# A decoder block in fp32 on one core: products weighed together per step, and an opening group in two halves of 256 tokens

## What is computed

```python
qkv = x @ w_atten.T                      # x: (4, 512, 512), normalised over its features
q, k = apply_rope(q, rope), apply_rope(k, rope)
att = jnp.einsum('bhqd,bhkd->bhqk', q, k) * (1.0 / jnp.sqrt(jnp.float32(D)))
att = jax.nn.softmax(jnp.where(causal, att, -inf), axis=-1)
y = jnp.einsum('bhqk,bhkd->bhqd', att, v)
return y @ w_proj.T
...
x = x + _L0_attn_ref(_layernorm(x), ...)
x = x + _L0_xattn_ref(_layernorm(x), ctx_1024, ...)
x = x + _L0_ffn_ref(_layernorm(x), ...)
```

## Time and profile before

| what | us |
|---|---|
| median of 3 runs | 1121.15 (1120.68 to 1123.51) |
| the profiled execution | 1121.97 |
| its span, first to last instruction | 1120.2 |
| TensorE busy | 1032.6 (92%) |
| VectorE busy | 600.2 (54%) |
| ScalarE busy | 482.6 (43%) |
| POOL busy | 180.6 (16%) |

### The profile page before, as it was taken

One profiled execution on the slowest core, in us unless ns is written; L12 is line 12 of the kernel. 1 busy time (PEld: TensorE's weight loads), 2 busy tenths in 40 slices (PEclk: granted clock), 3 DMA queues, 4 the chain that ended last, 5 costly groups with the idle time before them and its releaser, 6 DMA issues.

```text
span 1120.2 us, 17685 instructions
## 1 busy us (share of the span) xinstructions
PE 1032.6 (92%) x6000; PEld 735.6 (66%) x6000; DVE 600.2 (54%) x1592; ACT 482.6 (43%) x1265; POOL 180.6 (16%) x204
## 2 busy tenths in 40 slices
PE   6577799999999999999889999989999999999998
PEld 3243454564545555555454778888888988889997
DVE  3345556675567765566556455824444334443665
ACT  1144565564554655545564223213344334442221
POOL 2111111122011111111100000101111111112342
PEclk9878899999999999999999999999999999999999
DMA  6664444316443355404623103164442444423554
GB/s 188 129 106 57 57 58 70 48 27 74 106 57 78 36 71 119 57 28 50 135 76 102 33 19 104 39 237 141 145 149 92 149 152 152 144 83 94 181 170 159
DMA packets 66153, 111.21 MB, mean 99 GB/s; under 512 B 5984, under 2 KB 26976, under 8 KB 66080
## 3 DMA queue, kind: packets, MB, share of 16 engines
q1 hardware_dynamic: 60480, 91.92, 35.4%
q0 software_dynamic: 5600, 18.35, 5.5%
HBM read 59.66 MB, written 25.43 MB: 76 GB/s over the span
## 4 chain that ended last, share of the span: by engine, by line
PE 68%; DVE 12%; DMA 10%; issue 5%; ACT 2%; POOL 2%; SPq 1%; DVEq 0%; ACTq 0%; POOLq 0%
PE ps L1122 20%; PE ps L1132 10%; DMA ks<-rope_b 8%; PE ps L886 8%; PE ps L928 5%; PE ps L951 3%; PE ps L968 3%; PE ps L1026 3%; PE ps L905 3%; PE ps L917 3%; DVE gu_lo L1414 2%; PE ps L1140 2%; PE ps L988 1%; DMA routed_x<-xn_d,table_cur 1%; PE ps L1110 1%
## 5 line engine op out<-in xcount | busy, mean ns | idle before, releaser
L1265 DVE CUSTOM_DVE_ANT_0 probs<-ps,mask 128x128 f32<-128x128 f32 (+3 forms) x256 | 123.8, 487 | 140.0 <-PE ps L917 126.5
L677 ACT COPY probsT<-ps 128x128 f32<-128x128 f32 (+3 forms) x256 | 108.8, 425 | 192.0 <-PE ps L928 190.0
L917 PE MATMUL ps<-ks,qs 96*128 96x256 f32 (+2 forms) x256 | 149.4, 586 | 33.9 <-DMA ks<-rope_b 23.9
L669 ACT ACTIVATE probs<-probs,nb 128x128 f32<-128x128 f32 (+3 forms) x256 | 145.7, 569 | 34.0 <-DVE nb L1270 33.1
L886 PE MATMUL ps<-xnT,wa_sb 128*128 128x512 f32 x256 | 129.3, 620 | 3.6 <-DVE rope_b L1248 3.0
L928 PE MATMUL ps<-ident,probs 128*128 128x128 f32 x640 | 120.3, 288 | 0.1
L773 ACT ACTIVATE sg<-ps 128x352 f32<-128x352 f32 x69 | 32.0, 464 | 168.4 <-PE ps L1122 167.6
L917 PEld LDWEIGHTS ps<-ks,qs 96*128 96x128 f32 x256 | 50.9, 199 | 79.2 <-issue 36.6
L1541 DVE TENSOR_TENSOR hidden<-sg,ps 128x352 f32<-128x352 f32 x69 | 35.8, 519 | 122.8 <-ACT sg L773 122.8
L928 PEld LDWEIGHTS ps<-ident,probs 128*128 128x128 f32 x640 | 77.1, 144 | 33.7 <-issue 28.7
L570 POOL TENSOR_TENSOR rope_a<-rope_a,sin_sb 128x512 f32<-128x512 f32 x32 | 40.8, 1274 | 347.3 <-DVE rope_a L1247 347.3
(11 more groups left out here) (157 smaller groups left out, 1908.6 us busy)
## 6 DMA issues: line engine op xcount, KB each, us to landing
gu_raw<-in_we SPq DMA_DIRECT2D x10, 1408.0 KB
y_d<-y_sb SPq DMA_DIRECT2D x37, 256.0 KB
qs<-rope_b SPq DMA_DIRECT2D x32, 256.0 KB, 5.1
ks<-rope_b SPq DMA_DIRECT2D x32, 256.0 KB, 7.5
shared_x<-xT_d SPq DMA_DIRECT2D x32, 256.0 KB
d_raw<-in_we SPq DMA_DIRECT2D x10, 512.0 KB
qs<-rope_a SPq DMA_DIRECT2D x16, 256.0 KB, 7.2
ks<-rope_a SPq DMA_DIRECT2D x16, 256.0 KB, 8.4
```

The lines of the kernel that those rows point to most:

```text
L669: nc.scalar.activation(pr, pr, ACT.Exp, bias=nb[:, n % 2, h:h + 1], scale=SCALE, accum_out=sums[:, n % 2, h:h + 1]).then_inc(exp_done, 1)
L677: nc.scalar.copy(probsT[n % 2][:, h, 0:w], ps[:, T_BANK + h % 2, 0:w]).then_inc(pT_done, 1)
L917: nc.tensor.matmul(ps[:, S_BANK + h % 2, 0:w], qs[:, G % 2, h, i * P:(i + 1) * P], ks[:, G % 2, h, 0:w], start=True, stop=True).then_inc(s ...
L1265: nc.vector.tensor_tensor_reduce(probs[n % TT][:, h, 0:w], ps[:, S_BANK + h % 2, 0:w], mask[:, TOKENS - w:], 1.0, LOWEST, ALU.add, ALU.max ...
```

## The change

Four things. **Weighing**: `weigh(n)` now does all blocks of a step at the place of head 1 (`WEIGH_HEAD`), where one block stood at each place from head 0 on. **The opening** works on tokens 0 to 255 and then 256 to 511: x tiles 0 and 1, both first weights and tables, then x tiles 2 and 3 on the queue; statistics, root, turning, projections, rope and stack in halves; value tile 0 alone ahead of the loop, tiles 1 to 3 on places 0 to 11. The stack of each half counts on a semaphore of its own; scores of step 0 wait for the first, those of step 2 for the second. **Places and banks of groups 1 to 4**: their queries and keys stand close together (`EARLY_QUERIES`, `EARLY_KEYS`), keys in a bank other than the queries'; the sums of group 1 stand on places 6 and 8, those of groups 2 and 3 on the second and fourth place of the group ahead of theirs, those of group 4 on places 49 and 51. In the later batches value tile 3 comes three places earlier. **The stack** of every group: the high parts are sent when they are cast (`rope_high`), the low part when it is there (`rope_done`). All parts of the weights stand in front of the first stack, as before; the loads that stood behind it now stand behind the stacks of groups 1 (second x), 2 (weights, biases, context) and 3 (third x).

```diff
+WEIGH_HEAD = 1
...
-VALUES = ((-5, -5, -3, -3), (8, 9, 10, 10), (11, 12, 12, 14), (27, 27, 28, 29))
-VALUE_COPIES = (-3, 10, 14, 29)
+VALUES = ((-5, -5, -3, -3), (8, 9, 10, 10), (11, 12, 12, 14), (24, 24, 25, 26))
+VALUE_COPIES = (-3, 10, 14, 26)
+
+EARLY_QUERIES = {1: (2, 2, 3, 3), 2: (-2, -2, -1, -1), 3: (-2, -2, -1, -1), 4: (45, 45, 46, 46)}
+EARLY_KEYS = {1: (4, 4, 5, 5), 2: (0, 0, 1, 1), 3: (0, 0, 1, 1), 4: (47, 47, 48, 48)}
+EARLY_RAW = {1: (4, 6), 2: (0, 2), 3: (0, 2), 4: (47, 49)}
+EARLY_SUM = {1: (6, 8), 2: (2, 4), 3: (2, 4), 4: (49, 51)}
+FIRST_VALUES = ((-1, -1, -1, -1), (0, 0, 1, 1), (7, 7, 8, 8), (10, 10, 11, 11))
+FIRST_VALUE_COPIES = (-1, 1, 9, 12)
...
-        FIRST_QK_BANKS = (QK_BANK, O_BANK)
-        FIRST_VALUE_BANKS = (T_BANK, T_BANK + 1, QK_BANK)
-        EARLY_VALUES = len(FIRST_VALUE_BANKS)
+        HALVES = (slice(0, TOKENS // 2), slice(TOKENS // 2, TOKENS))
+        FIRST_QK_BANKS = ((QK_BANK, O_BANK), (T_BANK, T_BANK + 1))
+        FIRST_VALUE_BANKS = (T_BANK, T_BANK + 1, QK_BANK, O_BANK)
+
+        def qk_bank(G, i):
+
+            if i and G <= GROUPS:
+                return O_BANK if G == 1 else X_BANK
+            return QK_BANK
+
+        def qk_places(G):
+
+            if G <= GROUPS:
+                return EARLY_QUERIES[G], EARLY_KEYS[G]
+            return (QUERIES, KEYS) if G % GROUPS else (FIRST_QUERIES, FIRST_KEYS)
+
+        def unit(G, i, half=0):
+
+            return 2 * G + i + 2 if G else 2 * half + i
+
+        def value_places(b):
+
+            return (FIRST_VALUES, FIRST_VALUE_COPIES) if b == 0 else (VALUES, VALUE_COPIES)
...
-            def stack_part(G, i):
-
-                stacks, parts = ((qs, (rope_b, rope_b, rope_a)), (ks, (rope_b, rope_a, rope_b)))[i]
-                sp.wait_ge(rope_done, 2 * G + i + 1)
-                for j, part in enumerate(parts):
-                    sp.dma_start(stacks[j * HDIM:(j + 1) * HDIM, G % 2, :, :].bitcast(F32),
-                                 part[i][:]).then_inc(stacked, 16)
+            def stack_high(G, i, half=0, cols=slice(0, TOKENS), done=stacked):
+
+                sp.wait_ge(rope_high, unit(G, i, half) + 1)
+                for j in ((0, 1), (0, 2))[i]:
+                    sp.dma_start((qs, ks)[i][j * HDIM:(j + 1) * HDIM, G % 2, :, cols].bitcast(F32),
+                                 rope_b[i][:, cols]).then_inc(done, 16)
+
+            def stack_low(G, i, half=0, cols=slice(0, TOKENS), done=stacked):
+
+                j = (2, 1)[i]
+                sp.wait_ge(rope_done, unit(G, i, half) + 1)
+                sp.dma_start((qs, ks)[i][j * HDIM:(j + 1) * HDIM, G % 2, :, cols].bitcast(F32),
+                             rope_a[i][:, cols]).then_inc(done, 16)
...
+            def load_wa(part):
+
+                first_col, past = WA_PARTS[part]
+                sp.dma_start(wa_sb[:, :, first_col:past], wa_v[:, :, first_col:past]).then_inc(wa_loaded[part], 16)
+
+            for t in range(TT // 2):
                 sp.dma_start(acc[:, t, :], x_v[0][:, t, :]).then_inc(x_loaded[t], 16)
-            wa_v = waT.rearrange("(c p) n -> p c n", p=P)
-            for part, (first_col, past) in enumerate(WA_PARTS):
-                sp.dma_start(wa_sb[:, :, first_col:past], wa_v[:, :, first_col:past]).then_inc(wa_loaded[part], 16)
-                if part == 1:
-                    sp.dma_start(cos_sb[:], cosT).then_inc(tables_loaded, 16)
-                    sp.dma_start(sin_sb[:], sinT).then_inc(tables_loaded, 16)
-            for i in range(2):
-                stack_part(0, i)
-            load_x(1)
...
+            load_wa(0)
+            load_wa(1)
+            sp.dma_start(cos_sb[:], cosT).then_inc(tables_loaded, 16)
+            sp.dma_start(sin_sb[:], sinT).then_inc(tables_loaded, 16)
+            for t in range(TT // 2, TT):
+                sp.dma_start(acc[:, t, :], x_v[0][:, t, :]).then_inc(x_loaded[t], 16)
+            for part in (2, 3, 4):
+                load_wa(part)
+            for half, done in enumerate((stacked_first, stacked)):
+                for i in range(2):
+                    stack_high(0, i, half, HALVES[half], done)
+                    stack_low(0, i, half, HALVES[half], done)
             X3_PLACE = 2 * PLACES + 18
             WEIGHTS_PLACE = group_start(ALL_GROUPS - 1) + ROPE_SUM[1]
             for place in range(DRAINED):
-                for G, i in units_at(place, FIRST_ROPE_SUM, ROPE_SUM):
-                    stack_part(G, i)
+                for G, i in units_at(place, EARLY_SUM, FIRST_ROPE_SUM, ROPE_SUM):
+                    stack_high(G, i)
+                    stack_low(G, i)
+                if place == group_start(1) + EARLY_SUM[1][1]:
+                    load_x(1)
+                if place == group_start(2) + EARLY_SUM[2][1]:
+                    for dst, src in ((wp_sb[:], wpT.rearrange("(c p) n -> p c n", p=P)),
...
+                                     (bias_sb[:, 0:1], bq), (bias_sb[:, 1:2], bk)):
+                        sp.dma_start(dst, src).then_inc(w_loaded, 16)
+                    load_context(0)
+                if place == group_start(3) + EARLY_SUM[3][1]:
+                    load_x(2)
...
+                times_sine(0, 0, half, HALVES[half])
+                times_sine(0, 1, half, HALVES[half])
+                low_of_sum(0, 0, half, HALVES[half])
+                low_of_sum(0, 1, half, HALVES[half])
...
+                        before = (G - 1, 1) if bank == X_BANK else (0, 1) if bank == O_BANK else (G, 0)
+                        pe.wait_ge(rope_raw, 2 * unit(*before) + 2)
...
+                        before = (unit(0, 0, 1), unit(0, 1, 1), unit(1, 0), unit(1, 1))[t]
+                        pe.wait_ge(rope_raw, 2 * before + 2)
...
+                if n == 0 and h == 0:
+                    pe.wait_ge(stacked_first, STACK)
+                if h == 0 and (i == 0 and G or n == 2):
...
-            def weigh(n, j):
+            def weigh(n):
 
                 G, i = divmod(n, TT)
                 b, g = divmod(G, GROUPS)
-                if j == 0:
-                    pe.wait_ge(pT_done, GH * n + GH)
-                    if i == 0 and G >= 1:
-                        pe.wait_ge(yT_done, G)
-                if g == 0 and j == i:
-                    pe.wait_ge(v_done, b * TT + j + 1)
...
-                if j == i:
-                    last.then_inc(pv_mm, 1)
+                pe.wait_ge(pT_done, GH * n + GH)
+                if i == 0 and G >= 1:
+                    pe.wait_ge(yT_done, G)
+                if g == 0:
+                    pe.wait_ge(v_done, b * TT + i + 1)
+                for j in range(i + 1):
+                    v = value_tile(b, j)
+                    for h in range(GH):
+                        last = nc.tensor.matmul(ps[h * HDIM:(h + 1) * HDIM, O_BANK, i * P:(i + 1) * P],
+                                                v[:, g, h * HDIM:(h + 1) * HDIM],
+                                                probsT[n % 2][:, h, j * P:(j + 1) * P],
+                                                start=(j == 0), stop=(j == i), skip_group_check=True)
+                last.then_inc(pv_mm, 1)
...
+            for half in range(2):
+                for t in (2 * half, 2 * half + 1):
+                    if half:
+                        pe.wait_ge(norm1.copied, t - 1)
+                    turn_tile(norm1, 0, t, X_BANK + t % 2)
+                pe.wait_ge(norm1.copied, 2 * half + 2)
+                for i in range(2):
+                    pe.wait_ge(wa_loaded[i], 16)
+                    project_qk(0, i, range(CC), FIRST_QK_BANKS[half][i], HALVES[half])
             pe.wait_ge(wa_loaded[2], 16)
-            for t, bank in enumerate(FIRST_VALUE_BANKS):
-                values(0, t, range(CC), bank)
+            values(0, 0, range(CC), FIRST_VALUE_BANKS[0])
...
-                if n is not None and h <= n % TT:
-                    weigh(n, h)
+                if n is not None and h == WEIGH_HEAD:
+                    weigh(n)
...
+                    dve.wait_ge(stacked_first, STACK)
...
+            def first_stats(half):
+
+                tiles = range(2 * half, 2 * half + 2)
+                for t in tiles:
+                    dve.wait_ge(x_loaded[t], 16)
+                    pass_wait(dve)
+                    tile_stats(norm1, 0, t)
+                dve.wait_ge(norm1.stats_made, 4 * half + 2)
                 pass_wait(dve)
-                tile_stats(norm1, 0, t)
-            variances(norm1, 0)
-            for t in range(TT):
+                for t in tiles:
+                    nc.vector.bn_aggr(norm1.mv[:, t, :], norm1.stats[:, t, :]).then_inc(norm1.stats_made, 1)
+                dve.wait_ge(norm1.stats_made, 4 * half + 4)
+                at = slice(2 * half, 2 * half + 2)
+                nc.vector.tensor_scalar(norm1.veps[:, at], norm1.mv[:, at, 1], EPS, None, ALU.add).then_inc(norm1.var_made, 1)
+
+            first_stats(0)
+            for t in range(2):
                 scale(norm1, 0, 0, t)
+            first_stats(1)
```

(12 more changed lines are left out.)

147 lines of the change are left out of this document (65 added, 82 removed).

## The result

| | before | after |
|---|---|---|
| median, us | 1120.91 (4 runs) | 1083.49 (4 runs, 1078.21 to 1085.78) |
| ratio, with its 95% interval | | 0.966 (0.9617 to 0.9703) |
| profiled execution / its span | 1121.97 / 1120.2 | 1078.21 / 1076.4 |
| TensorE busy | 1032.6 | 1010.6 |
| TensorE not busy | 87.6 | 65.8 |

The change is worth 37 us by the medians; the forecast was 1078. Half of these is time in which TensorE stood still (21.8 us), and half (22.0 us) is TensorE's own busy time. Of busy time the prediction had only some 5 us: the half clock that it took out of groups 1 to 3 (7.0 us), less 1.6 for one start.

The account below looks back on a forecast made before the run. Latency sets the time up to S4, TensorE's own work behind it. Gains of 35.9 (to S4), 7.0 (weighing) and 1.3 (last batch's stack), 44.2 from 1121.97 us, give 1078 us; range 1068 to 1090, chance 0.60.

Parts of the forecast that it names:

- S0: First scores of group 0, ending the opening: forecast at 22.9 us, 15.0 earlier than before.
- group 0: From the first scores of group 0 to those of group 1: 29.0 us, with the next stack's transfer finishing last.
- group 1: From its first scores to those of group 2: 23.5 us, two equal limits, next stack and TensorE's work.
- group 2: From its first scores to those of group 3: 26.0 us, from 33.43 less 4.39 of waiting and 3.0 of half clock.
- S4: First scores of group 4: forecast at 124.0 us instead of 159.9, a gain of 35.9 that reaches the end.
- The half stack: Opening's first stack transfer, half the bytes: 6.3 us plus 1.8 for start and landing, 8.1 us.
- rival 3: A half stack transfer takes as long as a whole one: S0 at 29.2, total 1084 us; chance 0.10.
- rival 2: Nothing arrives at the end: loads behind the stacks or a second-batch wait replace the gain, 1120 us; chance 0.05.
- rival 1: Only the opening shrinks; exchange between scores, VectorE and ScalarE paces the groups: gain of 24, 1098 us; chance 0.20.
- not one product more or less; only the order changes: Weighing at one place: waits ahead of the weighing products fall, 8.8 us behind S4 less 1.8 cost, 7.0 gained.
- Rival 4: Slower: weighing bunched at one place keeps other work waiting, 41 us over all groups, 1127 us; chance 0.05.
- Of the other twelve stacks none was waited for.: High parts sent ahead of POOL's subtraction shorten only the last batch's stack wait, 1.3 us; twelve stacks stay hidden.

Follow-up runs that it names:

- the products in front: The changed kernel with ten identity products added ahead of the opening, while x is on its way; median 1074.54 us, ratio 0.957.
- products in its gaps: The changed kernel with sums of groups 2 and 3 one place later and eight unread filling products at places 18 to 37; median 1074.47 us.

## Why the prediction was right, and where it was wrong

| | forecast | after | |
|---|---|---|---|
| S0 | 22.9 | 25.5 | +2.6 |
| group 0 | 29.0 | 29.5 | +0.5 |
| group 1 | 23.5 | 26.3 | +2.8 |
| group 2 | 26.0 | 30.8 | +4.8 |
| group 3, with 1.6 for a start at half clock | 22.6 | 23.2 | +0.6 |
| S4 | 124.0 | 135.3 | +11.3 |
| S4 to the end | 952.0 | 941.1 | -10.9 |

(The forecast of the last line is 960.3 less 7.0 and 1.3.) The second profile of the kernel after has S4 at 137.3, so the mark that the prediction set for itself, 136, is touched: of the two parts of the sum the first was wrong, though the total was not.

That the total came out is luck, and more of it than the table shows. With the weighing spread again, the forecast by its own terms is 1077.8 + 7.0, that is 1085; measured were 1106, and S4 at 144.3 where 124.0 was forecast. So all that the forecast priced besides the weighing is some 21 us short, and the weighing, 7.0 forecast and 23 measured, made up 16 of them.

**Right.** What bounded the kernel, and that S4's gain reaches the end: nothing behind it took it back (with the weighing spread, S4 is 15.6 us sooner and the end 15.8). The half stack: 8.1 forecast, 7.8 measured, so its fixed cost comes once for six queued transfers; rival 3 (14 us, S0 at 29) is out, although its 1084 is nearer to the median than the forecast is. (The "six times 2 us" of the prediction do not give its "near 29" either: 14.75 and 12 are 26.8, and with the 6.3 of the bytes 33.) Group 0, whose length the transfer of the next stack sets. The stack waits at 8.0. That no load behind the stacks was missed: rival 2 is out.

**The opening, a term mis-sized.** Queries and keys of a half were put at 1.72 us each, half of what they took before at full clock. They took 5.49 together instead of 3.44, since TensorE had stood still until 7.25; before, it was at full clock by the time of its projections, with four tiles turned ahead of them (first turn at 10.23, projections at 14.64). Shown by the products in front: 3.72, and S0 at 23.20. The page's clock row shows full speed there, since the trace's first record of the clock comes only at 13.5 us; the durations show the half clock. The third tile of x was put at 8.5 and was measured from 9.43 on. The start of the projections came at 9.87, as forecast at 9.9, though the terms named there add up to 9.3.

**Groups 1 and 2, the step that failed.** I took out the clock's share of before and let one start at half clock stand, 1.6 us in all. The clock got worse instead: 0.81 and 0.83 against 0.93 and 0.91 before. What stands ahead of it: key raw and query sum at one place, with a sum slowed by POOL, and in group 2 the second batch's means behind them, hold the maxima and with them the scores by 2.48 us in group 1 and 3.76 in group 2, and TensorE then works 10 us at half clock in each group. I had taken VectorE as free, busy 18.5 of some 23 us, and did not write out the order on its queue at the places that had got new work. With the sums a place later group 1 lasts 23.9, close to the 23.5 of the forecast. Group 2 stays at 29.6 and at half clock for 10 us, behind a wait of 1.50; only with products in its gaps as well is it at full clock and 27.2 long. So the order on VectorE's queue is shown as the cause in group 1, and in group 2 half clock is shown as a part of the length; how long a group without either would be was not run.

That a stack wait that disappears would be followed by a wait for maxima is near to rival 1's mechanism, and its S4 of 136.0 was nearly what came. But its terms were not: its group 0 has 37.0 us, and 29.5 came. In groups 1 and 2 its 24.6 and 29.0 were nearer to the 26.3 and 30.8 measured than the forecast's 23.5 and 26.0. And 9.0 us of the measured S4 come from a gain which neither rival 1 nor the forecast had; with the weighing spread groups 1 and 2 last 29.8 and 33.0.

**Weighing, "not one product more or less; only the order changes".** The sentence is true and the inference wrong: time of products depends on their neighbours. 7.0 was forecast from waits alone. Measured on top of the rest: 23 us, while TensorE's busy time falls by 24.5 (18.1 in the weighing products themselves, compared with before). Of the waits alone, head 1 against head 0, some 5 arrive. The earlier trace rows showed a block of eight in 0.43 us, and no row of the kernel before has a second block behind it; I priced a bunched block at the same 0.43. This should have been called an operation that the trace does not show, with a range that reaches to a gain. Rival 4 took the bunching as slower by 41 us; the waits for maxima behind S4 did not appear (0.5 us there, 13.2 in the whole kernel), and it is out.

**"Of the other twelve stacks none was waited for."** True of the kernel before, and the wrong kernel to ask. Once TensorE's work is shorter they are no longer all hidden: high parts ahead of POOL's subtraction are worth 11 us, against the 3 to 4 that the forecast's terms make together, and 12.5 of the 15 us between the profiled executions lie behind S4.

The terms also don't add. Weighing 12 and the rest 15, each alone, make 27; together they make 37 to 39. A sum of parts, each priced against the kernel before, misses these 10 us.

What stays open: how much of the 8 to 9 us by which runs of the kernel after differ comes from the half-clock stretches behind S4 (283, 420 and 508 us after; 550, 577 and 755 before), what sets where those fall, and what brings the half clock in group 2 with the sums a place later.

## What to carry to other kernels

Small products that fill only a part of the array belong behind each other, as many as the buffers allow: the order alone was worth 2% here, and no row of a kernel that spreads them shows it. Before trusting a forecast in which waits disappear, write out the queue of every engine for the places that get new work, and ask again of each hidden transfer whether the shorter work still hides it. Ten products that nobody reads, ahead of TensorE's first work, were worth 8 us by the medians. In gaps of 2.5 to 3.8 us in the middle they cost nothing, and whether they gain depended on the order around them; the same products in a dense place cost their whole length.
